# A 128-column transpose stage cut in two: the first four token tiles are normalised, transposed, split and multiplied ahead of the last four

## What is computed

```python
xn = _layernorm(x, axis=-1)
s = _L0_attn_ref(xn, ...)          # NF4 weights with LoRA: q + k + v, o, then a gated MLP
g = _silu(_L0_ffn_ref(xn, w1, mean_w1, w2, mean_w2, w3, mean_w3))

def _binary_diff_weight(w, base):
    d = w - base
    coeff = jnp.mean(jnp.abs(d))
    return base + coeff * jnp.sign(d)

gate = jnp.einsum('bsh,ih->bsi', hidden_states, W1)      # W1, W2, W3 from _binary_diff_weight
up = jnp.einsum('bsh,ih->bsi', hidden_states, W3)
return jnp.einsum('bsi,hi->bsh', jax.nn.silu(gate) * up, W2)
```

## Time and profile before

| | |
|---|---|
| median of three executions | 536.0 us (535.98, 536.0, 536.23) |
| the profiled execution's own time | 536.4 us |
| its span, first to last instruction | 534.6 us |
| mean granted TensorE clock in the span | 0.997 |
| PE busy | 522.1 us, 98% of the span |
| DVE busy | 442.0 us, 83% |
| ACT busy | 328.5 us, 61% |
| POOL busy | 94.8 us, 18% |

### The profile page before, as it was taken

How to read it: one execution, slowest core, us unless ns; L and a number is a source line. 1 busy time by engine, 2 the same in 40 slices (tenths; PEclk the granted TensorE clock), 3 DMA queues, 4 the chain that set the end, 5 groups by cost and what they waited for, 6 DMA issues and landing times.

```text
span 534.6 us, 6499 instructions
## 1 busy us (share of the span) xinstructions
PE 522.1 (98%) x2337; PEld 432.2 (81%) x2337; DVE 442.0 (83%) x520; ACT 328.5 (61%) x455; POOL 94.8 (18%) x106
## 2 busy tenths in 40 slices
PE   5899999999999999999999999999999999999997
PEld 4678888888888888888888888887888888888886
DVE  6988998988896998865898988999989898874446
ACT  2979978557546555446648557867876585464310
POOL 1311002003100310022003121300310040004590
PEclk9899999999999999999999999999999999999999
DMA  8999904045811491059238994932582377127503
GB/s 337 397 402 403 377 4 154 25 132 99 189 50 63 70 229 58 1 104 224 51 75 159 243 219 100 195 83 63 97 163 58 75 157 148 29 51 161 135 20 139
DMA packets 31744, 76.73 MB, mean 144 GB/s; under 512 B 3872, under 2 KB 7296, under 8 KB 31584
## 3 DMA queue, kind: packets, MB, share of 16 engines
q1 hardware_dynamic: 21632, 57.42, 34.4%
q0 software_dynamic: 9792, 18.88, 20.4%
q10 hardware_dynamic: 288, 0.02, 0.0%
HBM read 53.23 MB, written 2.10 MB: 103 GB/s over the span
## 4 chain that ended last, share of the span: by engine, by line
PE 87%; DVE 8%; issue 3%; DMA 1%; ACT 1%; SPq 0%; DVEq 0%; ACTq 0%
PE up_ps L1692 25%; PE gate_pair L1692 22%; PE down_pair L1733 10%; PE up_ps L1733 9%; PE down_ps L1733 7%; PE side_ps L1776 2%; PE down_pair L1692 2%; DVE acc L1339 2%; PE down_pair L1645 1%; PE up_ps L1853 1%; PE gate_pair L1853 1%; PE down_pair L1853 1%; DMA xn<-in_x 1%; PE down_pair L1815 1%; PE gate_pair L1733 1%
## 5 line engine op out<-in xcount | busy, mean ns | idle before, releaser
L1692 PE MATMUL up_ps<-xT,gu 128*128 128x512 f32 x648 | 152.3, 390 | 0.4 <-DVE gu L1173 0.2
L1692 PE MATMUL gate_pair<-xT,gu 128*128 128x512 f32 x624 | 148.4, 390 | 0.0
L1692 PEld LDWEIGHTS up_ps<-xT,gu 128*128 128x128 f32 x648 | 121.4, 188 | 26.4 <-DVE gu L1173 0.6
L1692 PEld LDWEIGHTS gate_pair<-xT,gu 128*128 128x128 f32 x624 | 117.0, 188 | 24.6 <-DVE gu L1164 0.5
L651 POOL DMA_DIRECT2D y<-y_part x64 | 55.3, 875 | 339.9 <-ACT y_part L815 338.7
L802 ACT ACTIVATE h<-up_ps 128x512 fp32r<-128x512 f32 x52 | 31.0, 597 | 111.1 <-DVE up_ps L1231 58.0
L861 ACT ACTIVATE ramp<-codes,bend_bias 128x1536 f32<-128x1536 uint8 x56 | 88.1, 1579 | 0.9 <-DMA codes<-in_codes 0.9
L1339 DVE SCALAR_TENSOR_TENSOR acc<-ramp,acc 128x1536 f32<-128x1536 f32 x42 | 73.7, 1754 | 4.4 <-ACT ramp L861 4.0
L1733 PE MATMUL down_pair<-h,dn 128*128 128x512 f32 x249 | 60.9, 389 | 0.0
L1733 PEld LDWEIGHTS down_pair<-h,dn 128*128 128x128 f32 x249 | 46.7, 188 | 9.8
L1236 DVE TENSOR_TENSOR h<-up_ps,h 128x512 fp32r<-128x512 f32 x52 | 35.8, 689 | 19.7 <-ACT h L802 19.4
(11 more groups left out here) (227 smaller groups left out, 648.1 us busy)
## 6 DMA issues: line engine op xcount, KB each, us to landing
y<-y_part POOLq DMA_DIRECT2D x64, 256.0 KB, 5.0
scale<-in_scales SPq DMA_DIRECT2D x28, 384.0 KB, 5.5
scan_w<-in_w SPq DMA_DIRECT2D x15, 512.0 KB, 10.9
base<-in_mean SPq DMA_DIRECT2D x9, 768.0 KB, 4.8
scan_mean<-in_mean SPq DMA_DIRECT2D x9, 512.0 KB, 9.7
silu_gate<-in_mean SPq DMA_DIRECT2D x6, 512.0 KB, 12.2
codes<-in_codes SPq DMA_DIRECT2D x14, 192.0 KB, 5.6
xn<-in_x SPq DMA_DIRECT2D x4, 512.0 KB, 4.9
```

The costliest lines, as they stand in the source:

```text
L1692: last = nc.tensor.matmul(ps[:, :], w[:, w_part, hc * P:(hc + 1) * P], xT[:, x_part, hc, th * HALF:(th + 1) * HALF], start=(hc == 0 and w_ ...
```

## The change

DVE normalises tiles 0 to 3 in one go, before the statistics of the second half. PE transposes them, and ACT and DVE split them before DVE finishes the inverse root of the second half. PE then starts `early_mean(0)` (the first mean product, for the first token half), and the transposes of tiles 4 to 7 stand inside it, one tile after every three matmuls. `early_signs(0)` moves ahead of `early_mean(1)`, and `early_signs(1)` ahead of `total(GATE)`. ACT and POOL make the mean's two parts earlier, and ACT makes the sum and the sign of unit 0 between the copies of tiles 5 and 6. The warm transposes stand in other places: 6, 3, 3, 3 while the low parts are made, 6 ahead of `total(GATE)` and 10 behind it. No computation is added or taken away apart from the warm transposes (32 before, 31 now).

```diff
-WARM = {-1: 12, 1: 8, 3: 5, 7: 7}
+WARM_LOW = [6, 3, 3, 3]
+WARM_TOTAL = [6, 10]
@@ POOL
             def early_low():
                 pool.wait_ge(gu_hi, 1)
-                pool.wait_ge(scan_diff, dve_tiles(1))
@@
             early_low()
             unit_subtract(0)
-            pool.wait_ge(xT_lo, 4)
+            pool.wait_ge(xT_lo, 5)
             unit_subtract(1)
@@ ACT
             root(0)
-            x_high(0)
-            x_high(1)
+            for t in range(HC):
+                x_high(t)
             root(1)
             nc.scalar.activation(stats[:, 0, 0:BENDS], bend_bias[:, :], ACT.Silu)
-            x_high(2)
-            x_high(3)
+            early_high()
             scan_signs(0)
-            early_high()
             x_high(4)
             x_high(5)
+            unit_sum(0)
+            early_sign()
             x_high(6)
             x_high(7)
             scan_signs(1)
-            unit_sum(0)
-            early_sign()
             sum_apart(2)
@@ DVE
             inverse_root(0)
-            normalise(0)
-            normalise(1)
+            for t in range(4):
+                normalise(t)
             statistics(1)
-            normalise(2)
-            normalise(3)
+            scan_subtract(0)
+            for t in range(4):
+                x_low(t)
             inverse_root(1)
-            scan_subtract(0)
             for t in range(4, TT):
                 normalise(t)
             scan_subtract(1)
-            for t in range(4):
+            for t in range(4, TT):
                 x_low(t)
-            x_low(4)
-            x_low(5)
             scan_subtract(2)
-            x_low(6)
-            x_low(7)
@@ PE
             pe.wait_ge(const_ready, 3)
-            warm(side_ps, WARM[-1])
-            for t in range(TT):
+            def transpose_tile(t):
                 pe.wait_ge(xn_ready, t + 1)
                 for c in range(HC):
                     last = nc.tensor.matmul(x_ps[t][:, c * P:(c + 1) * P], xn[:, t, c * P:(c + 1) * P], ident[:],
                                             is_transpose=True, start=(c == 0), stop=(c == HC - 1))
                 last.then_inc(xT_tr, 1)
-                if t in (1, 3):
-                    warm(side_ps, WARM[t])
-            pe.wait_ge(xT_lo, 1)
-            warm(early_ps[0], WARM[TT - 1])
@@ in early_mean, for each hc
+                    if th == 0:
+                        transpose_tile(HC + hc)
@@
+            for t in range(HC):
+                transpose_tile(t)
+            pe.wait_ge(scan_diff, dve_tiles(0))
+            for low, count in enumerate(WARM_LOW):
+                if low > 0:
+                    pe.wait_ge(xT_lo, low)
+                warm(side_ps, count)
             early_mean(0)
+            early_signs(0)
             early_mean(1)
-            early_signs(0)
+            early_signs(1)
+            warm(side_ps, WARM_TOTAL[0])
             total(GATE)
-            early_signs(1)
+            warm(gate_ps[1], WARM_TOTAL[1])
```

## The result

The changed kernel takes 538.24 us, median of five runs (537.99 to 539.43), against 536.02 for the kernel before (535.98 to 536.23). The ratio is 1.0042, with an interval of 1.003 to 1.0054: slower by 0.4%. The profiled execution took 538.1 us with a span of 536.2; that of before took 536.4.

A forecast was written before the change was run, and what follows sets the result against it. PE, busy 98% of the span, was taken as the bound, so the end moves with the start of its dense stretch. Coefficient 1.7 later less 0.2 gave +1.5 on 536.4, so 537.9, median 537.5 us; range 536.5 to 538.6.

The forecast's parts named there:

- Transposes of tiles 0 to 3: PE's 16 transposes in a row from 9.22 us, 0.22 apart, the last ending at 12.95.
- The clock is up at 17.8: TensorE's clock, not yet up at 14.5 us, is up at 17.8, so the first mean product runs at full clock.
- rival (b): First mean product starts at the low clock, about 1 us more lost by tile 7: +2.5, 538.5 us; chance 0.10.
- The small operation waits for POOL: In DVE's second inverse root, a small operation waits up to 0.98 us for POOL's subtraction of unit 0; 0.58 at PE.
- Rival (a): DVE's small operations don't wait for POOL: the 0.58 is gone, +0.9, 536.9 us; chance 0.25.
- The step of 1.22: In the first mean product, each later tile waits for three matmuls (0.77) and four transposes (0.45): 1.22 us.
- ACT's sums stand behind the copy of tile 7: On ACT, scan tile 1 and all later sums follow that copy (23.45 us); the last sum ends at 31.12.
- The coefficient: Behind the gate scan's total, the coefficient starts at 31.75 us against 30.06, 1.7 later.
- What comes back at project(2): PE's wait at 37.95 us goes, as DVE's subtraction starts at 37.3, clear of POOL's operation: 0.2 back.
- Own time: Time of the profiled execution: 536.4 us plus 1.5, so 537.9.
- The median of the runs stands 0.4 under it: Last step of the sum: from the profiled execution's 537.9 us to a median of 537.5.
- Rival (c): The clock falls in PE's waits around the total, costing 1.7 us: +3.2, 539.2 us; chance 0.08.

The follow-up runs named there:

- e11: e9 with the total ahead of early_signs(1), unit_signs(1), (2) ahead of scan_signs(2), and spare transposes re-placed (eight, one, twelve behind tile 3); median 535.95 us.
- e4: Changed kernel with 18 more warm transposes right behind those of tile 3; no run time given, coefficient 0.21 us sooner in the profile.
- e6: Changed kernel with 12 and 16 spare transposes around the total instead of 6 and 10; seven of eight runs at 537.84 to 538.20 us.
- e2: Changed kernel with POOL's subtractions of units 1 and 2 right behind scan tile 1's; no run time given, coefficient moved by 0.09 us.
- e7: Changed kernel with the moves of e1 and e3, and ACT's sum and sign of unit 0 ahead of the copy of tile 4; 537.14 to 537.37 us.
- e3: Changed kernel with tiles 4 to 7 transposed in one go behind the first three matmuls; median 0.3 us lower.
- e10: Kernel before with 14 spare transposes instead of 7 ahead of its first mean product; median 536.03 us against 536.05.
- e5: Changed kernel without the sixteen spare transposes around the total; all six runs at 539.48 us or above.
- e1: Changed kernel with POOL subtracting unit 0 ahead of the low part of the mean; three runs at 537.02 to 537.68 us, four at 539.9 to 540.2.
- e9: e8 with scan_subtract(2) ahead of x_low(6), and no spare transposes ahead of the total (sixteen behind it); median 536.37 us.
- e8: e7 plus the move of e2, 12 and 16 spare transposes, and ACT's sums ahead of the sign of scan tile 2; no run above 537.4 us.

## Why the prediction was right, and where it was off

It forecast 537.5 us, slower than before; 538.24 was measured, slower, inside the range of 536.5 to 538.6 and 0.74 above the forecast. The chain that it named, from the small operation beside POOL over the copy of tile 7 to ACT's last sum, is the one that the profile shows. By its own steps:

- **Transposes of tiles 0 to 3:** 12.95 forecast, 12.90 measured, by luck: they began 0.24 late (9.46 for 9.22), and the last ones took 273 ns and not 421, since the clock rose at 12.6. DVE was 0.45 later than forecast at the subtraction of scan tile 0 (13.69 for 13.24). 0.15 of it was there at the first normalise (8.77 for 8.62), and 0.30 is the four normalises, which took 2.21 us beside POOL's copy, against 1.91. The sum had no term for that; in e11, where the copy began at 10.05, they took 1.92.
- **The clock is up at 17.8:** wrong, and it cost nothing in this profile. It was up at 12.6, fell at 16 and came back at 19.4; the first three matmuls took 1.65. Tile 4 was not there anyway (e4). So the condition of rival (b) was met for those three matmuls, and its price was not paid: the steps from tile 4 on were at full clock. That 538.24 lies close to its 538.5 is chance. What it costs when the clock stays low to 23.1 shows in the profile of e6: tile 7 came 1.52 later.
- **The small operation waits for POOL:** right. 0.98 was the upper bound, 1.02 was measured (1.18 less 0.16). Taking it away gave 0.69 at the coefficient, 0.53 without the earlier start; the forecast had 0.58. Rival (a) is out.
- **The step of 1.22:** 1.16 measured ((23.08 - 19.61) / 3). The copy of tile 7 began at 23.71 for 23.45.
- **ACT's sums stand behind the copy of tile 7:** right. From that copy to the last sum it was 7.69 us (31.40 - 23.71), forecast 7.67; e2 shows that DVE was not last, and e7 that the chain moves when ACT is fed: there DVE's last reduction waited 1.74 for ACT and still began 1.35 sooner. The test of the spreading alone, e3, did not show it.
- **The coefficient:** 32.17 for 31.75. Of the 0.42, 0.26 was there at the copy of tile 7 and 0.28 at the last sum (31.40 for 31.12); 0.14 came between the last sum and the coefficient. The 0.26 is what is left of the 0.46 by which tile 4 was late (19.61 for 19.15), DVE's 0.45, after three steps that were about 0.06 shorter each.
- **What comes back at project(2):** 0.37 (2.11 - 1.74) for 0.2, and for the reason given: DVE's scan subtraction at 37.67 took 1.22 us, clear of POOL's (34.48 to 35.78). The forecast took only the 0.21 of idle time. Idle time is counted from the end of project(1), and without it project(2) starts 0.17 before that end (39.69 for 34.12 + 5.74), so the distance of the two starts went from 5.94 to 5.57. The loads held too: POOL's subtraction of unit 4 came at 34.48 for 34.42.
- **Own time:** 538.1 for 537.9.
- **"The median of the runs stands 0.4 under it":** this step was off. The 0.4 was carried over from the profile of before to the changed kernel. The changed kernel's median is no lower than its profile, and 0.46 of delay at the coefficient, which e10 took away, belonged to the low clock in the profile of before. Against the median of before the profile of after is 2.1 longer, not 1.7.
- **Rival (c), the clock falls around the total:** not in the profile of after, but shown in those of e2, e4 and e5, at 1.5 to 1.6 us each (project(1) 7.22 to 7.36 for 5.74); the forecast had 1.7 and a chance of 0.08. One run of five of the changed kernel, at 539.43, would fit; it was not profiled. The chance was set too low. The chances for slower add up to 0.68 (0.50, 0.10 and 0.08), not 0.67.

**Left open:** which execution gets which clock; what puts four of seven runs of e1 at 540 (mean clock 0.997 in each; none was profiled, and e6's profile shows one way to lose 2.4) and five of eleven of e9 at 537.2 (mean clock 1.000 in each); and which of TensorE's two pauses, ahead of the total or behind it, lets the clock fall. They were 1.01 and 0.83 us in the changed kernel. The runs point at the one ahead, without showing it: e7 had 0.33 and 0.83, and none of its eleven runs was high, and in the profile of e6, with 0.35 and 1.03, project(1) ran at full clock; in the profiles of e2 and e4, with 1.00 ahead, it did not.

## What to carry to other kernels

Work that is moved into the gaps of one engine makes its consumer a follower: here ACT's copies came one by one behind the matmuls, and the sums queued behind them carried the delay to the point that decided. Look for what stands behind the last moved piece in the program of each engine. And before a profiled time is set against a median, see in which of its own modes (here the clock over one product) that execution ran.

## What the runs showed of the hardware

- An operation on 128x4 values of DVE with two inputs in SBUF waited until POOL's operation was over. In the profile of after it ran from 17.59 to 18.77, 1.18 us for 0.16, with POOL's ending at 18.74. In e11 it took 0.91 and ended at 17.88, with POOL's ending at 17.86; in e8 and e9 it took 0.26 and 0.24 and ended at 17.49, with POOL's ending at 17.47. DVE operations with an input in PSUM ran beside POOL unslowed, as the two low parts in the timeline of DVE in e8, beside POOL's subtraction at 21.06 (1.31):

```profile
20.90 1.28 DVE L1126 TENSOR_TENSOR xT<-gate_pair,xT 128x512 fp32r<-128x512 f32 x2
```

- POOL's operation is held up too: 2.21 us at 26.25 for 1.28, beside the two scan subtractions, which took 3.45 for 2.35. In e7 the same subtraction of unit 2 took 3.95 us, 24.52 to 28.47, and it was DVE that went unslowed, with its two scan subtractions (24.36, 2.35) and the unit subtraction behind them (26.63, 0.68); ACT then waited 0.28 for POOL. Which of the two pays is not the same from program to program.
- The clock rose while PE had done nothing but 128x128 fp32 transposes: at 12.6 in the profile of after, where one took 421 ns before and 273 ns behind.
- The instant at which the clock falls and comes back was not the same in executions of like programs: low from 16 to 19.4 in after and from 16.2 to 23.1 in e6, which are one program up to 29.9 us; and in e2, which differs up to there in two operations of POOL, only from 34.2 to 37.5.
